# Two sets of row maxima, and the first maxima of the next pair ahead of the turn of this pair's

## The reference

```python
q = jnp.concatenate([q_content, q_rope], axis=-1)
k = jnp.concatenate([k_content, k_rope], axis=-1)
scores = jnp.einsum('bhqd,bhkd->bhqk', q, k) * scale
scores = jnp.where(causal[None, None], scores, jnp.float32(-jnp.inf))
attn = jax.nn.softmax(scores, axis=-1)
out = jnp.einsum('bhqk,bhkd->bhqd', attn, v)
```

## Time and profile before

| | before |
|---|---|
| median of three runs | 1501.66 us (1500.64 to 1509.76) |
| the profiled execution | 1515.03 us, of which its span is 1513.2 us |
| TensorE matmul, busy share of the span | 82% |
| VectorE, busy share of the span | 74% |
| mean granted clock of TensorE | 0.893 |
| first attention: first and last boundary | 73.3 and 788.0 us |

### The profile page before, as it was taken

How to read it: one execution, slowest core, us unless ns; L and a number is a source line. 1 busy time by engine, 2 the same in 40 slices (tenths; PEclk the granted TensorE clock), 3 DMA queues, 4 the chain that set the end, 5 groups by cost and what they waited for, 6 DMA issues and landing times.

```text
span 1513.2 us, 40070 instructions
## 1 busy us (share of the span) xinstructions
PE 1247.5 (82%) x14676; PEld 892.7 (59%) x14676; DVE 1114.4 (74%) x3616; ACT 815.7 (54%) x1971; POOL 685.6 (45%) x1042
## 2 busy tenths in 40 slices
PE   4499889988899988999988899589989998647780
PEld 2255545555455554555556899467777777547660
DVE  5588687886878868888665665558788878755666
ACT  1155555555555555555555455178787657326663
POOL 3023241233432334323223654466666768674664
PEclk9699999999999999999999899777887757668995
DMA  5656727556275572755741311022111112222335
GB/s 120 108 96 91 115 29 117 87 92 107 30 121 81 91 115 28 119 81 91 119 181 35 102 47 30 25 69 63 46 45 44 35 34 76 99 68 81 89 85 173
DMA packets 73892, 123.37 MB, mean 82 GB/s; under 512 B 17534, under 2 KB 46083, under 8 KB 72800
## 3 DMA queue, kind: packets, MB, share of 16 engines
q1 hardware_dynamic: 63896, 104.97, 36.6%
q0 software_dynamic: 7616, 13.59, 2.8%
q10 hardware_dynamic: 2184, 2.25, 0.8%
HBM read 30.40 MB, written 17.60 MB: 32 GB/s over the span
## 4 chain that ended last, share of the span: by engine, by line
PE 43%; DVE 28%; POOL 9%; ACT 8%; issue 6%; DMA 3%; ACTq 1%; DVEq 1%; SPq 0%; POOLq 0%
DVE first L843 7%; PE A L640 6%; DVE S L846 4%; PE S L1099 4%; PE S L611 4%; PE S L622 4%; PE S L1659 3%; DVE tA L822 3%; POOL xq L1468 2%; PE A L1670 2%; PE A L1106 2%; DMA Qp<-mT 2%; DVE tB L823 2%; PE S L1645 2%; PE S L1676 2%
## 5 line engine op out<-in xcount | busy, mean ns | idle before, releaser
L727 ACT ACTIVATE P<-S 128x512 f32<-128x512 f32 (+3 forms) x768 | 330.6, 491 | 285.6 <-PE S L622 283.3
L622 PE MATMUL S<-Qp,Kp 121*128 121x512 f32 (+3 forms) x768 | 258.2, 394 | 39.1 <-DMA Qp<-mT 11.8
L907 POOL TENSOR_SCALAR_AFFINE_SELECT P<-P 128x256 f32<-128x256 f32 x256 | 112.6, 443 | 373.8 <-ACT P L727 373.1
L846 DVE CUSTOM_DVE_ANT_0 S<-S,later 128x512 f32<-128x512 f32 (+3 forms) x512 | 238.9, 514 | 53.7 <-PE S L611 52.4
L611 PE MATMUL S<-Kp,Qp 120*128 120x512 f32 (+3 forms) x768 | 243.4, 389 | 30.7 <-DMA Kp<-big 16.3
L622 PEld LDWEIGHTS S<-Qp,Kp 121*128 121x128 f32 x768 | 137.4, 190 | 123.9 <-DVE first L843 24.6
L843 DVE TENSOR_REDUCE first<-S 128x1 f32<-128x512 f32 x256 | 164.3, 682 | 55.0 <-PE S L611 54.5
L611 PEld LDWEIGHTS S<-Kp,Qp 120*128 120x128 f32 x768 | 132.9, 194 | 112.5 <-issue 49.7
L640 PE MATMUL A<-P,V 128*9 128x256 f32 (+1 forms) x2816 | 174.5, 343 | 5.4 <-POOL P L907 4.6
L640 PEld LDWEIGHTS A<-P,V 128*9 128x9 f32 x2816 | 63.9, 90 | 70.9 <-issue 29.8
L1896 POOL TENSOR_TENSOR prod<-mid,kT 128x128 f32<-128x128 f32 x160 | 68.0, 459 | 72.1 <-ACT mid L1727 45.4
(11 more groups left out here) (358 smaller groups left out, 2585.7 us busy)
## 6 DMA issues: line engine op xcount, KB each, us to landing
Qp<-big SPq DMA_DIRECT2D x63, 256.0 KB
Kp<-big SPq DMA_DIRECT2D x62, 256.0 KB
Qp<-big SPq DMA_DIRECT2D x63, 128.0 KB
Kp<-big SPq DMA_DIRECT2D x62, 128.0 KB
xq<-xq SPq DMA_DIRECT2D x71, 72.0 KB
yb<-yq SPq DMA_DIRECT2D x8, 528.0 KB, 7.2
big<-in_w SPq DMA_DIRECT2D x4, 1024.0 KB, 9.9
big<-vt SPq DMA_DIRECT2D x32, 128.0 KB
```

The costliest lines, as they stand in the source:

```text
L622: te.matmul(S[s][:, 512 * h + c:512 * h + 512], K[0:121, h, 128 * kb:128 * kb + 128], Q[0:121, h, 512 * qh + c:512 * qh + 512], start=True ...
L727: se.activation(k.P[(w.n - 1) % NP0][:, h, c:512], S[s][:, 512 * h + c:512 * h + 512], ACT.Exp, scale=SCALE0).then_inc(p.done("st").h, 1)
L846: ins = ve.tensor_tensor_reduce(out=of, in0=of, in1=k.later[:, 512 - n:512], scale=1.0, scalar=-3e38, op0=ALU.add, op1=ALU.max, accum_out= ...
L907: ge.affine_select(P[:, :, c:c + 128], P[:, :, c:c + 128], [[0, 2], [1, 128]], ALU.is_ge, 0.0, base=0, channel_multiplier=-1).then_inc(p.s ...
```

## The change

There are now two tiles `mx` and two `first`, used in turn by even and odd pairs, and the list has the first "mx" item of pair u+1 ahead of the turn of pair u's maxima. On VectorE the wait of a pair's maxima for the transposition of the pair before becomes one for the pair before that.

```diff
-        self.mx, self.first, self.mT = sb("mx", [128, 2, 8]), sb("first", [128, 2, 4]), sb("mT", [16, 128], F32R)
+        self.mx, self.first, self.mT = [sb(f"mx{i}", [128, 2, 8]) for i in range(2)], [sb(f"firsts{i}", [128, 2, 4]) for i in range(2)], sb("mT", [16, 128], F32R)
...
         def maxima(u, i):
 
+            if u < NU:
+                o.add("mx", u, *pieces[i], ring="S")
             if i == 0 and u > 0:
                 o.add("mxT", u - 1, ring="S")
-            if u < NU:
-                o.add("mx", u, *pieces[i], ring="S")
...
-            te.transpose(S[s][0:16, 0:128], k.mx[:].rearrange("p h n -> p (h n)"), p.ident[:]).then_inc(p.made("mxT").h, 1)
+            te.transpose(S[s][0:16, 0:128], k.mx[w.at[0] % 2][:].rearrange("p h n -> p (h n)"), p.ident[:]).then_inc(p.made("mxT").h, 1)
...
-            if u:
-                dve.wait_ge(p.made("mxT"), u)
-            n = 128 * (qt + 1) - 512 * part
+            if u > 1:
+                dve.wait_ge(p.made("mxT"), u - 1)
+            n, mx = 128 * (qt + 1) - 512 * part, k.mx[u % 2]
```

More of the change, by code:

```diff
@@ L842, in attn0_vector @@
                 if part == 0 and qt >= 4:
-                    ve.tensor_reduce(k.first[:, h, qt - 4:qt - 3], S[s][:, 512 * h:512 * h + 512], AX.X, ALU.max).then_inc(p.done("mx").h, 1)
+                    ve.tensor_reduce(k.first[u % 2][:, h, qt - 4:qt - 3], S[s][:, 512 * h:512 * h + 512], AX.X, ALU.max).then_inc(p.done("mx").h, 1)
                     continue
@@ L846, in attn0_vector @@
                 ins = ve.tensor_tensor_reduce(out=of, in0=of, in1=k.later[:, 512 - n:512], scale=1.0, scalar=-3e38, op0=ALU.add, op1=ALU.max,
-                                              accum_out=k.mx[:, h, qt:qt + 1])
+                                              accum_out=mx[:, h, qt:qt + 1])
                 if qt == 0 and h == 1:
                     dve.then(ins)
-                    ins = ve.tensor_tensor(k.mx[:, :, 4:8], k.mx[:, :, 4:8], k.first[:], ALU.max)
+                    ins = ve.tensor_tensor(mx[:, :, 4:8], mx[:, :, 4:8], k.first[u % 2][:], ALU.max)
                 ins.then_inc(p.done("mx").h, 1)
```

## The result

The changed kernel takes **1530.42 us** (median of four runs, 1525.47 to 1535.38) against 1501.15 us (four runs, 1498.44 to 1509.76): ratio **1.0176 [1.0138, 1.0214]**, slower. The forecast was 1522 us, in a range of 1503 to 1541.

The account below looks back on a forecast made before the run. TensorE and VectorE, neither full, hand PSUM tiles round a ring of three, and the DMA of the maxima is already late. Boundary delays, less small gains, plus one clock fall sum to 20.6 us: 1501.66 + 20.6, about 1522 us, range 1503 to 1541.

Parts of the forecast that it names:

- The selects on GpSimd: Two causal selects behind the DMA in GpSimd's queue: held up, but ending at 260.2, ahead of their reader at 261.91; cost nothing.
- The first rival: VectorE's idle time before the reduction is really won: up to 18.5 us less, 1483 us; chance 0.10.
- first boundary: Pair 0 to 1: the transposition stands behind pair 1's item, which waits for its keys; first scores later, +2.9 us.
- eight clear boundaries: Boundaries waiting for the DMA, clear of the start and the rotation: each 1.45 us later, 11.6 us in all.
- the short waits: Places where VectorE's reductions were nearly as late as the DMA: delay shortened by about 0.33, three times, -1.0 us.
- four beside the rotation: Boundaries where VectorE's 0.64 wait for GpSimd's rotation takes part of the 1.29 delay: 4 x 0.65 = 2.6 us.
- seven quiet: Boundaries without query and key loads beside them: 0.48 to spare, 0.8 late, half absorbed by the ring: 2.8 us.
- eleven others: Remaining boundaries showing no wait for the DMA: bounds 0 to 16 us, taken as one full delay, 1.4 us.
- the two transpositions: Two steady-part boundaries where the transposition waits for the join L850, holding the next pair's matmuls: gain 2 x 0.56, -1.1 us.
- the clock: TensorE's granted clock falls behind longer waits: one more fall counted, +1.4 us, bounds none to 14.
- the second rival: Most of the DMA's delay is hidden where load bursts held it up: 1 to 12 us, 1503 to 1514; chance 0.22.
- The third rival: Every long wait drops TensorE's clock, at some ten boundaries: 33 us, up to 40, 1535 to 1541; chance 0.08.

## Why the prediction was right

**The mechanism** held at each step. The reduction did not start earlier (0.47 against 0.48 behind the product; the bound was 0.2), the negation came at 1.67 (forecast 1.75), the scores' wait went to 36.6 at 26 (forecast 30 to 40 at 18 or more), and the late issue by itself, in the old order, gives the whole loss. The selects on GpSimd cost nothing, as it said: TensorE's products waited for them 4.0 us at 5 places, and 4.6 at 6 before. The first rival, that the idle time is won, fell with the list of waits and with the two sets in the old order: the tiles changed nothing. By the rule in the Trainium skill, Perfetto Trace Analysis, Optimization Strategy, a repeating gap can mean too few buffers; here 18 equal gaps stayed at 21.0 us with twice the buffers.

**The sum**, against the growth of the start of each pair's first score item (its first matmul), after less before, from one boundary to the next. By pair 31 it is 25.8, of which 2.9 were there at the start; the rows are rounded:

| term | forecast | measured |
|---|---|---|
| first boundary | 2.9 | 3.7 (6.6 less the 2.9) |
| eight clear boundaries, less the short waits | 10.6 | 6.6 |
| four beside the rotation | 2.6 | 4.3 |
| seven quiet | 2.8 | 0.8 |
| eleven others, less the two transpositions | 0.3 | 5.8 |
| the clock; measured: growth from pair 30 to the last boundary | 1.4 | 1.6 |
| sum | 20.6 | 22.9 |

The sum is nearly right because its errors cancel, which is luck. *The eight clear boundaries were taken too high.* A later issue did not simply land later there. Pair 7's DMA took 4.39 us to its scores before (237.89 to 242.28), and took 2.79 when issued 1.6 later, so the boundary lost nothing:

```profile
249.10 0.51 POOL L901 DMA_DIRECT2D Qp<-mT  x1 [2.09 <-DVE mT L857]
...
251.90 0.30 PEld L622 LDWEIGHTS S<-Qp,Kp 121*128 121x128 f32 x2 [1.33 <-DMA Qp<-mT]
```

Pair 29 lost nothing either (-0.2), while pair 8, where the time grew from 2.79 to 4.07, lost 2.65. That is the second rival, true at some of them; how far pair 8 is the opposite, and how far scatter, is open (4.40 with nothing late, above).

*The seven quiet ones were taken too high as well.* Their spare time, 0.48, was read from the last boundary's 2.40. At six of them the DMA, issued 1.2 later, was taken up 1.72 to 1.74 after its issue (2.88 to 2.89 before), with a wait of 0.26 to 0.29. Pair 14:

```profile
425.60 0.52 POOL L901 DMA_DIRECT2D Qp<-mT  x1 [2.02 <-DVE mT L857]
...
427.34 0.19 PEld L622 LDWEIGHTS S<-Qp,Kp 121*128 121x128 f32 x1 [0.29 <-DMA Qp<-mT]
```

So nearly the whole delay was spare there, and only pair 10 paid for it (1.0). Two larger steps in this row almost cancel: pair 18 gave back 1.5, behind pair 17's 1.7, and pair 26 has 1.4, behind two falls of the clock. The rotation's 4.3 is the other side of the first; its four range from 0.5 to 1.7.

*The eleven others were taken too low*: 1.4, one full delay for all, between bounds of 0 and 16. Pairs 3, 4, 11, 12 and 27 alone grew by 0.8 to 1.5 each, 5.7 together: a boundary that shows no wait had spare time, but less than the delay. Pairs 5, 13, 19 and 21 took it for 0.3 or less. The two transpositions that waited for the join gave 0.28 and 0.22 and not 0.56.

**The clock** was taken too low, and its row in the table holds the last fall alone. From 90 us to the last transposition the granted clock is at the lower level in seven stretches of the kernel after, 27.3 us in all, and in two of the kernel before, 6.8 us. Two of the seven, and one of the run with two sets in the old order:

```profile
563.00:566.50 3.50, 3.50 (x21) 1.94 (x21) 0.97 (x2) 0.58 (x4) 0.41 (x1) 0.51 0.73 117
686.00:689.50 3.50, 3.50 (x7) 2.26 (x8) 1.21 (x5) 1.09 (x2) 1.74 (x2) 0.52 0.00 0
```

```profile
547.50:551.00 3.50, 3.50 (x21) 1.80 (x21) 0.88 (x2) 0.54 (x3) 0.41 (x1) 0.53 0.70 117
```

What one costs is read from runs with and without it at the same place. From its first scores to the product ahead of the next boundary's turn, pair 8 takes 18.9 us with a fall (after) and 17.4 to 17.8 in the runs that have none there, pair 29 takes 15.7 (before) against 14.3 to 14.6, pair 30 takes 16.2 (after) against 14.4 to 14.7; but pair 17 takes 23.3 either way (before, and two sets in the old order). Where only one of the two kernels has a fall, the change's differences are +1.1 (pair 8), +1.4 (pair 25), +1.8 (pair 30), +0.2 (pair 11), +1.4 (at the boundary of pair 20) and -1.4 (pair 29): 4.5 us of the growth, an estimate, where the forecast had 1.4. It is spread over the other rows of the table.

The third rival fell all the same, since not every long wait dropped the clock: the weight load's waits of 2.70 at pair 16 and 1.67 at pair 29 had no fall behind them. Nor does every fall stand behind a wait for the DMA: the one at 563 has none over 0.3 ahead of it since pair 17, and the run with two sets in the old order has one at the same work (547). The Trainium skill, TensorE: Matmul & The Clock Gate, HAM oscillation, ties such falls to waits for a DMA; pairs 8, 25 and 30, with waits of 2.62, 2.24 and 4.74, agree, and pairs 16, 20 and 29 don't. What decides it stays open.

**The level.** Ratio times median is 26.4 us and the difference of medians 29.3; the stage shows 23.0. The interval of the ratio is 20.7 to 32.1 us, so the forecast's 20.6 stands just below its lower end.

## What to carry to other kernels

Before moving an instruction to fill an idle gap, look what else stands behind the instruction that ends it: here the reduction and the transposition stood behind the same product, so the gap had to stay whatever the order. Of two instructions that become ready together, the one that starts the longer chain to a waiting reader goes first, even if it is the short one that makes the busy engine look idle. And a place without a wait in the profile is not yet a place with enough spare time: here eleven such places lost 5.8 us together, a little over a third of the full delay of 1.4 each, and seven quiet ones 0.8.

## What the runs showed of the hardware

The same 8 KB DMA was taken up 1.74 us after its issue at pair 14, took 2.26 us in the chain at the last boundary, and 6.16 at pair 30, behind the issue of the next layer's weights (L535, L536). The busy times by engine of these last two stretches, pair 30's first, show the DMA engines busy throughout at 421 GB/s, and nearly idle at 11:

```profile
790.90:797.10 6.20, 1.93 (x21) 0.78 (x19) 2.34 (x6) 0.45 (x2) 1.27 (x3) 0.85 1.02 421
814.80:817.00 2.20, 2.18 (x27) 1.37 (x25) 0.00 (x0) 1.32 (x5) 1.30 (x3) 1.00 0.04 11
```

Its time isn't a constant that a later issue shifts (4.39 and then 2.79 at pair 7), nor is it the same in two executions of one order (2.79 and 4.40 at pair 8). Averaged over 31 boundaries the stage still lost 0.6 to 0.7 us for each us of delay, over mean delays of 0.9 to 3.4 us; what the clock took is in this.
